# A gated cross-attention and feed-forward layer on one core: the output bias moves from a TensorE product to GpSimd and ScalarE, and the hand-written order of five engines changes

## What is computed

```python
x = x + tanh(g_xattn) * xattn(layernorm(x), ctx, ctx)   # 16 heads of 64, causal softmax, out @ Wo
h = layernorm(x)                                        # the input of the block below
# ffn block of h: for each token 16 heads of 8 attend to each other
q = (rmsnorm(h)*g1) @ Wq + bq; k, v = split(((..) @ Wdown + bdown) @ Wup + bup)
o = softmax(q k^T / sqrt(8)) v                          # within one token
x2 = h + (o @ Wo + bo)
h2 = rmsnorm(x2)*g2; gate = softmax(h2 @ Wg + bg)       # 8 experts
x = x + tanh(g_ffn) * (x2 + sum_e gate[e] * (h2 @ We[e]))
```

## Time and profile before

| what | value |
|---|---|
| median of 3 runs | 260.2 us (260.14 to 263.66) |
| the profiled execution, its own time | 261.93 us |
| its span in the profile | 259.9 us |
| mean granted clock of PE | 0.993 of full speed |
| busy, share of the span | PE 94%, PEld 69%, DVE 74%, ACT 66%, POOL 58% |

### The profile page before, as it was taken

How to read it: one execution, slowest core, us unless ns; L and a number is a source line. 1 busy time by engine, 2 the same in 40 slices (tenths; PEclk the granted TensorE clock), 3 DMA queues, 4 the chain that set the end, 5 groups by cost and what they waited for, 6 DMA issues and landing times.

```text
span 259.9 us, 7887 instructions
## 1 busy us (share of the span) xinstructions
PE 245.6 (94%) x3244; PEld 178.7 (69%) x3244; DVE 192.4 (74%) x333; ACT 171.6 (66%) x501; POOL 149.9 (58%) x157
## 2 busy tenths in 40 slices
PE   7989989998899999999999999988999897979995
PEld 4765877785867677676859595858676462858774
DVE  0237644189998989898998842799989999786964
ACT  2437634756687787978787778566877676472454
POOL 4104041264646686969696835778466995867320
PEclk9999999999999999999999999999999998899999
DMA  6990000000000000000000000000000000000000
GB/s 208 359 320 21 3 4 3 3 1 3 3 3 0 3 10 3 15 0 15 1 3 13 3 11 3 13 3 10 3 0 5 11 14 3 11 0 3 10 13 20
DMA packets 6017, 7.30 MB, mean 28 GB/s; under 512 B 477, under 2 KB 4830, under 8 KB 5982
## 3 DMA queue, kind: packets, MB, share of 16 engines
q1 hardware_dynamic: 5550, 6.16, 7.5%
q10 hardware_dynamic: 432, 0.64, 0.7%
HBM read 5.88 MB, written 0.92 MB: 26 GB/s over the span
## 4 chain that ended last, share of the span: by engine, by line
PE 70%; DVE 18%; ACT 5%; issue 4%; POOL 1%; DVEq 0%; POOLq 0%
PE ps_a L875 40%; PE ps_c L875 9%; PE ps_b L875 8%; PE ps_e L875 7%; PE ps_b L927 4%; DVE ps_e L665 3%; DVE prod L683 3%; DVE ps_e L694 2%; ACT probs L446 2%; DVE nmax L626 2%; PE ps_b L872 1%; DVE psums L631 1%; DVE fqkv L649 1%; POOL prod L326 1%; PE ps_c L971 1%
## 5 line engine op out<-in xcount | busy, mean ns | idle before, releaser
L326 POOL TENSOR_TENSOR prod<-fqkv 128x1280 f32<-128x1280 f32 (+1 forms) x14 | 38.7, 2761 | 10.3 <-DVE fqkv L649 10.3
L316 POOL TENSOR_TENSOR probs<-probs,prinv 120x672 f32<-120x672 f32 x16 | 24.3, 1518 | 31.1 <-DVE prinv L635 31.1
L334 POOL TENSOR_TENSOR prod<-e_sb,fqkv 128x768 f32<-128x768 f32 (+1 forms) x14 | 24.5, 1753 | 21.3 <-ACT e_sb L474 21.3
L875 PEld LDWEIGHTS ps_a<-aT,wo_sb 128*128 128x128 f32 x256 | 30.8, 196 | 4.4 <-ACT v_sb L435 2.6
L875 PE MATMUL ps_a<-aT,wo_sb 128*128 128x112 f32 x256 | 32.1, 279 | 0.4 <-ACT aT L440 0.3
L875 PE MATMUL ps_a<-wv_sb,cT 128*64 128x512 f32 x128 | 32.3, 620 | 0.0
L665 DVE TENSOR_REDUCE ps_e<-prod 128x256 f32<-128x2048 f32 x13 | 29.7, 2287 | 0.0
L694 DVE TENSOR_REDUCE ps_e<-prod 128x128 f32<-128x2048 f32 x13 | 29.7, 2285 | 0.0
L875 PE MATMUL ps_a<-cT,wk_sb 128*128 128x224 f32 x128 | 28.6, 375 | 0.0
L429 ACT COPY kT<-ps_a 128x448 f32<-128x448 f32 x32 | 17.1, 533 | 16.2 <-PE ps_a L875 16.2
L875 PE MATMUL ps_a<-xT,wqc 128*128 128x224 f32 x128 | 27.1, 361 | 0.6 <-ACT qT L429 0.6
(11 more groups left out here) (144 smaller groups left out, 487.9 us busy)
## 6 DMA issues: line engine op xcount, KB each, us to landing
xp_sb<-in_xp SPq DMA_DIRECT2D x1, 896.0 KB, 7.9
out<-out_sb SPq DMA_DIRECT2D x14, 64.0 KB, 1.5
xT<-in_x_t SPq DMA_DIRECT2D x1, 784.0 KB, 9.5
cT<-in_ctx_t SPq DMA_DIRECT2D x1, 784.0 KB, 11.1
wv_sb<-in_wv SPq DMA_DIRECT2D x1, 512.0 KB, 8.1
wo_sb<-in_wo SPq DMA_DIRECT2D x1, 512.0 KB, 12.7
fwe_sb<-in_fwe SPq DMA_DIRECT2D x1, 512.0 KB, 8.8
fw_sb<-in_fw SPq DMA_DIRECT2D x1, 266.0 KB, 13.1
```

Source lines behind the costliest of these rows:

```text
L316: nc.gpsimd.tensor_tensor(pr[0:TG, NC:C, :, 0:S], pr[0:TG, NC:C, :, 0:S], prinv[p % 2][0:TG, NC:C, :].unsqueeze(3).to_broadcast([TG, C - N ...
L326: nc.gpsimd.tensor_tensor(o, k, q, ALU.mult).then_inc(s["prod1_pool"], 1)
L334: nc.gpsimd.tensor_tensor(o, e, v, ALU.mult).then_inc(s["prod2_pool"], 1)
L875: return nc.tensor.matmul(o, lhsT, rhs, start=start, stop=stop, skip_group_check=True)
```

## The change

1. `bias_o` goes. ACT scales the centred x in place (`scaled_x`, xc times rstd2), POOL adds the bias to it in place (`biased`), and DVE's `new_x2` becomes a plain addition that also waits for POOL (`ub_ready`).
2. The calls stand in a new order on PE, DVE, POOL and ACT, in both loops and in the last stretch.

The diff's pieces, in this order: `biased` on POOL, `scaled_x` on ACT, `new_x2` on DVE, ACT's first loop, ACT's second loop (steps 14 and 15).

```diff
+            def biased(f):
+                pool.wait_ge(s["u_ready"], f + 1)
+                if f == 0:
+                    pool.wait_ge(s["wo_scaled"], 2)
+                nc.gpsimd.tensor_tensor(xc[f % XB][:, :], xc[f % XB][:, :], fw_sb[:, COL_BO:COL_BO + D], ALU.add).then_inc(s["ub_ready"], 1)
...
+            def scaled_x(f):
+                act.wait_ge(s["centred"], f + 1)
+                act.wait_ge(s["rstd2_ready"], f + 1)
+                nc.scalar.activation(xc[f % XB][:, :], xc[f % XB][:, :], ACT.Copy, scale=rstd2[f % XB][:, 0:1]).then_inc(s["u_ready"], 1)
...
             def new_x2(f):
                 dve.wait_ge(s["o_made"], f + 1)
-                nc.vector.scalar_tensor_tensor(out=x2[f % 2][:, 0:D], in0=xc[f % XB][:, :], scalar=rstd2[f % XB][:, 0:1], in1=ps_c[:, 1, 0:D],
-                                               op0=ALU.mult, op1=ALU.add).then_inc(s["x2_ready"], 1)
+                dve.wait_ge(s["ub_ready"], f + 1)
+                nc.vector.tensor_tensor(x2[f % 2][:, 0:D], ps_c[:, 1, 0:D], xc[f % XB][:, :], ALU.add).then_inc(s["x2_ready"], 1)
...
+                if fc is not None:
+                    o_copy(fc)
                 if t < NP:
                     values(t, 0)
-                if fc is not None:
-                    o_copy(fc)
+                    values(t, 1)
+                if fb is not None:
+                    scaled_x(fb)
                 if t < NP:
                     exps(t)
-                    values(t, 1)
...
                 values(t, 0)
+                values(t, 1)
+                gate_exps(fc)
+                head_exps(fb)
                 turned_probs(t)
-                values(t, 1)
-                head_exps(fb)
+                scaled_x(fb)
                 x1_copy(fa)
-                gate_exps(fc)
```

The second loop gets the same moves on POOL; on DVE `logits` goes ahead of `prob_sums` and `new_x1` behind `shifted_logits`; on PE one values half goes behind `shift` and `new_o`. In the last stretch DVE now forms `products(last)` behind `shifted_logits(prior)`:

```diff
             products(prior)
+            scaled_qkv(last)
             new_x2(third)
-            scaled_qkv(last)
+            shifted_logits(prior)
             products(last)
-            shifted_logits(prior)
             weighted(prior)
```

More of the change, by code:

```diff
@@ L378, in _ @@
                     products(fb)
+                if fd is not None:
+                    outputs(fd)
+                if fc is not None:
+                    second_scale(fc)
                 if t < NP:
                     norm(t)
-                if fc is not None:
-                    second_scale(fc)
                 if fb is not None:
                     weighted(fb)
+                if fc is not None:
+                    gating(fc)
                 if fa is not None:
                     first_scale(fa)
-                if fc is not None:
-                    gating(fc)
-                if fd is not None:
-                    outputs(fd)
+                if fb is not None:
+                    biased(fb)
             for t in range(TAIL, END):
@@ L408, in _ @@
             gating(third)
+            biased(prior)
             weighted(last)
             second_scale(prior)
+            biased(last)
             gating(prior)
+            last_residual(last)
             second_scale(last)
-            last_residual(last)
         @block.scalar
@@ L536, in _ @@
                 fa, fb, fc = (TILE_AT.get(t - k) for k in range(3))
-                if t < NP:
-                    values(t, 0)
                 if fc is not None:
@@ L541, in _ @@
                 if t < NP:
+                    values(t, 0)
+                    values(t, 1)
+                if fb is not None:
+                    scaled_x(fb)
+                if t < NP:
                     exps(t)
-                    values(t, 1)
                 if fc is not None:
@@ L585, in _ @@
             o_copy(third)
+            scaled_x(prior)
             x1_copy(last)
+            squares(third)
             kv_copy(last)
             x2_copy(third)
-            squares(third)
             head_exps(prior)
@@ L592, in _ @@
             gate_exps(third)
+            scaled_x(last)
             head_exps(last)
+            experts(third, 0)
+            o_copy(prior)
             experts(third, 1)
-            o_copy(prior)
-            experts(third, 0)
+            x2_copy(prior)
             squares(prior)
-            x2_copy(prior)
-            late_out(third)
             o_copy(last)
             gate_exps(prior)
+            late_out(third)
             squares(last)
             x2_copy(last)
+            experts(prior, 1)
             experts(prior, 0)
-            experts(prior, 1)
             gate_exps(last)
@@ L798, in _ @@
                     new_x2(fc)
-                if t < NP:
-                    prob_sums(t)
+                if fb is not None:
+                    logits(fb)
                 if t <= NP:
@@ L859, in _ @@
             gate_logits(prior)
+            new_x2(last)
             gate_sum(prior)
-            new_x2(last)
             gate_logits(last)
@@ L971, in turn_o, with new_o @@
                 nc.tensor.transpose(ps_c[:, 0, 0:128], onorm[f % 2][:, :], ident[:, :]).then_inc(s["o_turned"], 1)
-            def bias_o(f):
+            def new_o(f):
+                if f == 0:
+                    pe.wait_ge(s["wo_scaled"], 2)
                 if f > 0 and f - 1 in BIG:
@@ L1094, in _ @@
                     scores(t)
+                if fc is not None:
+                    turn_o(fc)
+                if t < NP:
                     values(t, 0)
@@ L1097, in _ @@
                 if fc is not None:
-                    turn_o(fc)
+                    new_o(fc)
                 if t < NP:
                     shift(t)
-                if fc is not None:
-                    bias_o(fc)
-                    new_o(fc)
                 if t <= NP:
@@ L1130, in _ @@
                 scores(t)
-                values(t, 0)
                 turn_o(fc)
                 shift(t)
-                bias_o(fc)
                 new_o(fc)
+                values(t, 0)
                 turn_x2(fc)
+                gate_logits(fc)
                 values(t, 1)
                 new_y(t - 1)
-                gate_logits(fc)
+                expert_half(fc, 1)
                 turn_probs(t)
                 first(fa)
+                attend(t)
                 expert_half(fc, 0)
-                attend(t)
-                expert_half(fc, 1)
             last, prior, third = NT - 1, NT - 2, NT - 3
@@ L1149, in _ @@
             first(last)
-            bias_o(third)
             new_o(third)
@@ L1153, in _ @@
             turn_x2(third)
+            expert_half(third, 0)
+            gate_logits(third)
             output_sums(PE_OUT[0])
-            gate_logits(third)
+            head_sums(prior)
             expert_half(third, 1)
-            head_sums(prior)
-            expert_half(third, 0)
             turn_o(prior)
-            bias_o(prior)
             new_o(prior)
@@ L1165, in _ @@
             turn_o(last)
-            bias_o(last)
             new_o(last)
+            expert_half(prior, 1)
+            turn_x2(last)
             expert_half(prior, 0)
-            turn_x2(last)
-            expert_half(prior, 1)
             gate_logits(last)
+            expert_half(last, 1)
             expert_half(last, 0)
-            expert_half(last, 1)
             output_sums(prior)
```

33 lines of the change are left out of this document (15 added, 18 removed).

## The result

The changed kernel takes 263.46 us (median of 19 runs, 262.56 to 264.62), the kernel before 260.14 us (19 runs): 1.012 times as long, 95% interval 1.010 to 1.014. I had said 261.2 us, so a loss of 1.0 where there is one of 3.3. The profiled execution took 262.82 us, with a span of 261.0.

What follows compares the result with a forecast made beforehand. It took PE to bound the steady steps, with DVE 1.3 us to spare. Terms +1.3 - 0.4 + 1.6 - 2.6 + 0.6 = +0.5 took the profiled 261.93 to 262.4 us; for the median it said 261.2, range 256.8 to 265.0.

Steps and rivals of the forecast that it cites:

- the clock: Tail of the kernel before: 1.1 us of its expected gain is a lower-clock stretch; the median might not have it.
- steps 5 to 8 and 13: Steady steps go from 13.91 to 14.2 us; 0.25 us charged for each of the five, +1.3.
- steps 9 and 10: Steps lacking fa and fb keep the gain of a bias product each: -0.4 us.
- steps 11 and 12: Called even: DVE's head exponentials come 1 us earlier in 11, PE gives it back waiting for onorm in 12.
- steps 3 and 4: Reduction waits for POOL's products, delaying x1T, projections and turn_probs; +1.6 us, bounds 0.6 to 2.6.
- step 14 to logit sums: Steps 14 and 15: new order brings tile 12's fqkv 2.6 us earlier, 1.1 of it not the order's.
- logit sums to the end: Last stretch: products(last) stands behind shifted_logits(prior), ahead of the weighting PE's head sums need; +0.6 us (0 to 1.2).
- the second projection's wait: Step 3: PE's second projection must wait for x1T, held behind the long reduction; 1.6 us.
- The bias product: Its removal saves PE 0.22 us a tile, 1.8 us over the eight steps where PE bounds.
- POOL is the later: PE waits at turn_probs: Steady step: POOL's queue delays the norm, PE waits 0.4 to 0.5 us. P is turn_o's start, Q scaled_qkv's end.
- The cover: ACT's added scaling (0.39 us) and POOL's addition (0.46) hide, done a step before x2: cost 0.
- Exclusion of DVE and POOL: Rival: DVE's norm waits up to 0.55 us beside POOL's outputs or second_scale; total 263.7 us, chance 0.06.

Runs made afterwards that it cites:

- second profile of before: The kernel before, unchanged, run once more for a profile: 260.29 us, span 258.4, clock 1.00 throughout.
- Run 10: The changed kernel with DVE's old order (long reduction behind the sums and x1T) in step 3 alone: 262.74 us, 1.010 of the kernel before.
- run 1: The kernel before with only the bias moved to ACT and POOL, every other call where it was: 261.27 us, 1.002 of the kernel before.
- 15: Old order, bias moved, new_y ahead of new_o, two projections ahead of turn_x2, ACT's first two projection copies earlier: 260.20 us, 1.000 of the kernel before.
- 16: The same orders as 15, but the bias product kept on PE, without ACT's scaling and POOL's addition: 261.14 us, 1.003 of the kernel before.
- run 9: The changed kernel with POOL's last two output additions behind the norm in the first loop: 263.67 us, 1.013 of the kernel before.
- run 14: The changed kernel with DVE's old order in step 3, and new_o between the two values halves on PE: 266.23 us, 1.022 of the kernel before.
- run 2: The changed kernel with the bias product back on PE and no scaled_x or biased, so the order alone: 266.90 us, 1.024 of the kernel before.
- run 7: The changed kernel with PE's old order (values, turn_o, shift, new_o) in the first loop: 266.36 us, 1.022 of the kernel before.
- run 4: The changed kernel with POOL's old order in the first loop (outputs ahead of products, second_scale behind the norm): 279.90 us, 1.075 of the kernel before.
- run 6: As run 5, with DVE's products(last) ahead of shifted_logits(prior) again: 263.61 us, 1.013 of the kernel before.
- run 5: First loop in the old order with the bias moved, second loop and last stretch in the new order: 261.65 us, 1.005 of the kernel before.
- run 3: The changed kernel with DVE's old order in the first loop (long reduction behind sums and x1T): 267.48 us, 1.027 of the kernel before.
- runs 8: As run 6, with turn_o between the two values halves and ACT's expert halves swapped: 263.27 us, 1.011 of the kernel before.
- experiment 11: Old order, bias moved, with new_y ahead of new_o and two projections ahead of turn_x2 in the first loop: 260.09 us, 0.998 of the kernel before.

## Why the prediction was right or wrong, point by point

The terms without the clock's, against the second profile of before where the tail is concerned:

| term | predicted | measured |
|---|---|---|
| steps 5 to 8 and 13 | +1.3 | +1.25 |
| steps 9 and 10 | -0.4 | +0.44 |
| steps 11 and 12 | 0 | +0.64 |
| steps 3 and 4 | +1.6 | +2.43 |
| step 2 | - | +0.16 |
| step 14 to logit sums | -1.5 | -2.15 |
| logit sums to the end | +0.6 | +0.60 |
| sum | +1.6 | +3.4 |

3.4 is near what the medians show (3.3); with the second profile of before for the loop too it is 3.1. Steps 6 and 8 of the first profile were 0.39 us longer than a steady step, else the first row would be +1.65, five times 0.33.

I said +1.0 and not the table's +1.6, because I took the middle between a median with the stretch at the lower clock and one without. That halving is 0.6 of the 2.3 us that I missed. The terms of the order are the rest: too low by 0.8 in steps 3 and 4, by 0.8 in 9 and 10, by 0.6 in 11 and 12 and by 0.2 in step 2, which I had left out, less 0.65 that the tail gained beyond my term. The sign was right, and the steady step (14.24 for "14.2"), the second projection's wait (1.29 for 1.6) and the last stretch came out.

- **The mis-sized terms** are those of the places where the pattern breaks. "Steps 9 and 10 keep the gain of a product each" and "steps 11 and 12 I call even" failed, by 0.84 and 0.64 us. In step 12 onorm starts 2.7 us after the step in both kernels (2.67, before 2.83). Before, PE did the values products in that time and went on 12.1 us later to the next step; now it stands 1.41 us with nothing ahead of turn_o, and from onorm to the next step it is 13.4. I had priced this wait for step 4 and let it go in 12. In step 10 turn_o starts 1.55 us after the step's start and not 1.14 as in step 7. These 0.41 us lie inside the scores: PE stops after 30 of the 64 products, and the profile names no engine that it waits for. The cause is open. Without this stop steps 9 and 10 together are 0.03 us longer than before, so the gain of the product is missing there too.
- **Steps 3 and 4** cost 2.43, inside my bounds (0.6 to 2.6). "Part of it comes back" was right for PE: from turn_probs to attend it took 2.46 us in step 3 (58.16 to 60.62) and takes 1.70 now (59.28 to 60.98). What I missed is that ACT's exponentials of the heads stand behind its copies of the projections, so that PE's stop hands them to DVE late (1.17 us of wait for 0.45), and onorm of step 4 with them. Run 10 shows what the reduction's place in step 3 has to do with it: 0.85 us.
- **The bias product** "0.22 us in the steps where PE bounds" was wrong for the steady steps of the old order (run 1: nothing) and right where no wait lies beside it (step 4 of run 1: 0.22; 15 against 16: 0.23). I had read a PE that is busy 13.91 of 13.91 us as one that waits for nothing. The product lay between two rows whose distance ACT's copy set. The Trainium skill, Perfetto Trace Analysis, "Identifying the Most-Contended Engine", calls matmul busy time a poor measure of how near PE is to its limit and looks at the weight loads; those were busy for 10.22 of the 13.91 us, which leaves room for slack, and run 1 agrees. The sign of it stood in the timeline of before: ACT's copy of oT ends 0.13 us ahead of new_o (shown with run 1).

- **The cause of the steady step**: "POOL is the later: PE waits at turn_probs" failed, run 9 excludes it. What sets the step is the path through PE and DVE: turn_o, values, new_o, x2, the long reduction, x1T, the sums, prinv, and from there the norm and turn_probs. Four runs moved the end of prinv and left POOL's queue idle ahead of the norm; the step moved with it, and from prinv to the end of the step it is always the same:

| kernel, step | POOL idle ahead of the norm | end of prinv after the step's start | step | difference |
|---|---|---|---|---|
| changed, 7 | 0.28 | 7.80 | 14.24 | 6.44 |
| run 14, 7 | 0.38 | 8.02 | 14.47 | 6.45 |
| run 2, 7 | 0.56 | 8.08 | 14.52 | 6.44 |
| run 7, 7 | 0.75 | 8.28 | 14.72 | 6.44 |
| run 4, 6 | 3.99 | 9.83 | 16.27 | 6.44 |

  I had DVE's path to prinv end near P + 6.6 and POOL free at Q + 7.1. Prinv ended at P + 6.66 (107.68 to 114.34), POOL was free at Q + 6.9 (107.26 to 114.13), and P was Q + 0.42: both within 0.25 us of each other, DVE the later. The wait of 0.4 to 0.5 at turn_probs is 0.25, with 0.13 at the projections. That the step came out near "14.2" is luck: the two paths happen to end together. With a wrong cause I would have mended the wrong queue.
- **The tail** gained 2.15 for 1.5, and with the last stretch's +0.6 as predicted. The +0.6 lies where I put it: products(last) now stands right ahead of esum, and esum starts 5.66 us after the logit sums where it started 5.07 after them (232.34 to 237.41 in the second profile). But the place of products(last) alone is not the cause. Put back (run 6) it makes that stretch 0.55 us longer, because in the new ACT order its input is later. What gained the 2.15 was not taken apart further than run 5 does.
- **The clock** cost 1.2 us in the tail of the profile of before, near my 1.1, but it is in only 22 of 97 runs of that kernel over five batches (in the last one 20 of 23 are at full clock with a median of 260.13, three below it with 261.7). So the median had none of it, and my other number, 261.8, was the one to take.
- **The cover** held: x2 never waited for POOL's addition. ACT's scaling takes 0.41 us, POOL's addition 0.46, and both hide.
- **Exclusion of DVE and POOL**: DVE loses nothing, its norm takes 392 ns on the mean, as before, and POOL's outputs are unchanged. But my "no row of the kernel before shows such a meeting" was wrong. DVE's part of the norm and POOL's start 0.05 us apart in nearly every step, before as now (111.14 here, 111.19 in the earlier trace rows), and POOL's then takes 1.52 us:

```profile
111.14 0.39 DVE L638 TENSOR_TENSOR probs<-probs,prinv 120x224 f32<-120x224 f32 x1
```

  In six steps of run 3 POOL's last addition of outputs starts just behind DVE's norm instead, and POOL's norm runs later and alone:

```profile
115.80 0.39 DVE L660 TENSOR_TENSOR probs<-probs,prinv 120x224 f32<-120x224 f32 x1
...
115.86 0.64 POOL L348 TENSOR_TENSOR out_sb<-exb 128x128 f32<-128x128 f32 x1
...
117.00 1.31 POOL L316 TENSOR_TENSOR probs<-probs,prinv 120x672 f32<-120x672 f32 x1
```

  POOL's addition, begun just behind DVE's, takes 0.64 us for its usual 0.46, in six steps alike (0.64 to 0.67), and POOL's norm takes 1.31 us for its usual 1.52. So the meeting stretches whichever POOL instruction it falls on by 0.2 us, and the changed kernel pays that on the path that sets its step. By the Trainium skill, SBUF — State Buffer, "Who interferes with whom", a DVE instruction with two SBUF inputs contends with a GpSimd one that reads SBUF; the traces agree, at a price of 0.2 us, paid by POOL.

## What to carry to other kernels

Before you price an instruction that goes, look at the distance between its neighbours and ask what sets it: a short product may stand in a wait for another engine's copy, and then it costs nothing. When an order moves, walk every step where the pattern breaks with the new order, and ask at each wait what the engine had been doing in that time before. An order of several engines is one thing: each part alone may be worse than both whole versions.

## What the runs showed of the hardware

- Splitting eight 512-column products into two halves with a 128-column one between cost about 0.15 us of PE a step, and turn_o took 0.16 us to the next start ahead of bf16 products and 0.26 ahead of fp32 ones of 512 columns (runs 8 and 14).
- The last two stores took 3.2 us from issue to landing in the profile of kernel 6, 3.0 in that of 3 and 2.6 in that of 8, and 1.5 in all others. The instructions are the same; I have no cause.
- Single steps came out 0.3 to 0.6 us longer in one profile and not in another of the same kernel (before: step 6 14.23 and 13.96, step 8 13.98 and 14.53). In both long steps the extra time lies inside the scores, and the profile names no engine that PE waits for.
- How often an execution has a stretch at the lower clock differs between the kernels: 0 of 12 runs in experiment 11, 6 of 12 in experiment 1, all six in 4 and 14.
